# Cross-attention on one core: scores formed transposed, row maxima exchanged through DRAM

## The reference

```python
a = layer_norm(ctx, gamma, beta)                  # (32, 375, 512)
Q = heads(x @ Wq.T)                               # (32, 16, 112, 32)
K = heads(a @ Wk.T); V = heads(a @ Wv.T)          # (32, 16, 375, 32)
scores = einsum('bhtd,bhsd->bhts', Q, K) * 32 ** -0.5
attn = softmax(where(mask, scores, -inf), axis=-1)
out = merge(einsum('bhts,bhsd->bhtd', attn, V)) @ Wo.T
return x + tanh(gate) * out
```

## Time and profile before

| | us |
|---|---|
| runs (3) | 1137.56, 1139.86, 1142.44; median 1139.86 |
| span of the profiled execution, first to last instruction | 1134.9 |
| PE busy / PEld busy | 1100.3 / 921.6 |
| DVE / ACT / POOL busy | 861.4 / 679.0 / 565.0 |

### The profile page before, as it was taken

How to read it: one execution, slowest core, us unless ns; L and a number is a source line. 1 busy time by engine, 2 the same in 40 slices (tenths; PEclk the granted TensorE clock), 3 DMA queues, 4 the chain that set the end, 5 groups by cost and what they waited for, 6 DMA issues and landing times.

```text
span 1134.9 us, 28841 instructions
## 1 busy us (share of the span) xinstructions
PE 1100.3 (97%) x9614; PEld 921.6 (81%) x9614; DVE 861.4 (76%) x2438; ACT 679.0 (60%) x1811; POOL 565.0 (50%) x745
## 2 busy tenths in 40 slices
PE   9799899999999999999999999999999999999997
PEld 8798788878888888888888888888888887888885
DVE  4643888887877788888787788888787778887764
ACT  2414565656666666666666666666666666666653
POOL 1344746555555566655455566655554566655100
PEclk9899899999999999999999999999999999999997
DMA  9453223222333233323333333323333333331000
GB/s 270 168 152 70 69 73 72 55 76 74 83 85 85 72 85 73 66 64 75 77 85 85 80 77 77 70 56 75 77 85 85 82 75 76 67 67 45 10 17 17
DMA packets 53010, 89.55 MB, mean 79 GB/s; under 512 B 15184, under 2 KB 35664, under 8 KB 52976
## 3 DMA queue, kind: packets, MB, share of 16 engines
q1 hardware_dynamic: 52400, 88.19, 31.8%
q10 hardware_dynamic: 576, 0.92, 0.3%
HBM read 81.66 MB, written 7.44 MB: 79 GB/s over the span
## 4 chain that ended last, share of the span: by engine, by line
PE 72%; DVE 16%; DMA 5%; issue 4%; POOL 1%; ACT 1%; SPq 1%; DVEq 0%; POOLq 0%
PE bank L690 43%; PE bank L747 14%; PE bank L847 6%; DVE shared_f L668 6%; PE bank L770 6%; DVE stats L574 4%; DVE shared_f L649 3%; PE bank L712 2%; DMA qT<-in_wkT 2%; DMA row_stats<-row_stat 1%; DMA rows<-in_ctx 1%; DVE mv L577 1%; POOL cn L404 1%; ACT shared_f L513 1%; DMA stat_bc<-row_stats 0%
## 5 line engine op out<-in xcount | busy, mean ns | idle before, releaser
L404 POOL TENSOR_TENSOR cn<-cn,stat_bc 128x375 f32<-128x375 f32 x256 | 258.8, 1043 | 387.4 <-DMA stat_bc<-row_stats 371.1
L513 ACT ACTIVATE shared_f<-shared_f,ntop 112x375 f32<-112x375 f32 x512 | 306.3, 601 | 14.3 <-DVE ntop L649 14.1
L690 PE MATMUL bank<-shared_r,w_k 128*128 128x376 f32 x1536 | 295.9, 342 | 0.0
L690 PE MATMUL bank<-w_v,shared_r 128*125 128x512 f32 x1152 | 291.7, 402 | 0.1
L649 DVE CUSTOM_DVE_ANT_0 shared_f<-bank,mask_b 112x375 f32<-112x375 f32 x512 | 258.6, 543 | 32.1 <-PE bank L770 30.8
L690 PEld LDWEIGHTS bank<-shared_r,w_k 128*128 128x128 f32 x1536 | 260.4, 190 | 0.3
L747 PEld LDWEIGHTS bank<-ident,shared_f 112*125 112x125 f32 x1536 | 199.1, 190 | 67.9 <-issue 27.9
L690 PEld LDWEIGHTS bank<-w_v,shared_r 128*125 128x125 f32 x1152 | 206.7, 186 | 46.1 <-issue 0.5
L668 DVE TENSOR_SCALAR shared_f<-shared_f,rden 112x375 f32<-112x375 f32 x512 | 240.3, 531 | 4.5
L747 PE MATMUL bank<-ident,shared_f 112*125 112x112 f32 x1536 | 222.1, 281 | 20.2 <-DVE shared_f L668 19.6
L536 ACT ACTIVATE shared_f<-bank 125x448 f32<-125x448 f32 x256 | 139.0, 543 | 166.8 <-PE bank L747 166.8
(11 more groups left out here) (49 smaller groups left out, 816.4 us busy)
## 6 DMA issues: line engine op xcount, KB each, us to landing
rows<-in_ctx SPq DMA_DIRECT2D x32, 750.0 KB
cn<-in_ctxT SPq DMA_DIRECT2D x32, 750.0 KB, 12.2
stat_bc<-row_stats SPq DMA_DIRECT2D x32, 375.0 KB, 4.4
xy<-in_x SPq DMA_DIRECT2D x32, 224.0 KB, 2.5
out<-xy SPq DMA_DIRECT2D x32, 224.0 KB, 2.3
shared_f<-in_xT SPq DMA_DIRECT2D x7, 896.0 KB, 8.9
mask_u<-in_mask SPq DMA_DIRECT2D x32, 41.0 KB, 3.1
qT<-in_wqT SPq DMA_DIRECT2D x4, 256.0 KB, 5.5
```

Source lines behind the costliest of these rows:

```text
L404: last = pool.tensor_tensor(chunk, chunk, stat_bc[:, w, :], op)
L513: last = act.activation(prob[0:T, r % 2, h, :], prob[0:T, r % 2, h, :], ACT.Exp, bias=ntop[0:T, r % 2, h:h + 1], scale=-1.0, accum_out=den ...
L690: last = pe.matmul(dst, l, m, start=(start and k == 0), stop=(stop and k == len(pairs) - 1))
```

## The change

The scores are formed transposed: the K chunk is the stationary operand and the query the moving one, 125 context positions on the partitions by 4 x 112 query columns, for each of the three thirds j (ST = 3). They are float32 products with the operands unsplit (`kT` and `qs` lose their low parts). The exponentials are then already in the form in which the weighted sum takes them, and the weights (probabilities) are never transposed. The maximum of a query now runs over partitions and thirds. ACT copies the scores with the mask as a bias. DVE takes the maximum within each quadrant of 32 partitions (a reduction with a transposed read), SP stores these 128 x 42 numbers to DRAM and loads them back so that each partition has all twelve (four quadrants by three thirds) for its 14 queries; DVE reduces these, spreads the result over the partitions with a transposed copy, and subtracts it. ACT takes the exponentials. PE sums them over all three thirds with a matrix of ones and puts the sums beside the weighted sum; the division is made once per element, on the heads' output. The split of that output into high part and rest is also made once per element, and the output projection comes later, in a slot of the second element after. V has two banks. The mask is loaded and transposed once. Rows, context and statistics are loaded in other slots of SP than before.

The core of the diff, in the order SyncE (the exchange and its slots), ScalarE (copies and exponentials), VectorE, TensorE (scores, the sums at the end of `weighted_sum`, the slot):

```diff
+        row_max = nc.dram_tensor("row_max", (32, HC * ST * BLK), F32, kind="Internal").ap()
...
+            def exchange_maxima(i, r):
+                sync.wait_ge(quad_max, i * LOOP + r)
+                sync.dma_start(row_max.rearrange("t (q k) -> q t k", q=HC), rmax[:, :]) \
+                    .then_inc(max_stored, 16)
+                wait_apart(sync, max_stored, i * (16 * LOOP) + r * 16)
+                sync.dma_start(x4[:, :], bass.AP(
+                    tensor=row_max.tensor, offset=0,
+                    ap=[[0, HC], [HC * ST * BLK, 32], [1, HC * ST * BLK]])).then_inc(ld_max, 16)
 
             def slot(i, r):
                 c, u = divmod(r, KT)
+                if live(i, LOOP, r - 1, SLOTS):
+                    exchange_maxima(i, r)
+                if u == 0:
+                    if live(i, 2, c + 3, B) and behind(i, 2, c + 1):
+                        store_stats(i, c + 3)
+                    if live(i, 2, c - 1, B) and not first_two(i, c - 1):
+                        wait_apart(sync, stored[(c - 1) % 2], i * 16 + (c - 1) // 2 * 16)
+                        load_x(i, c - 1)
+                if u == 2:
+                    if live(i, 2, c + 3, B) and behind(i, 2, c + 1):
+                        load_stats(i, c + 3)
+                    if live(i, 2, c + 3, B) and not first_two(i, c + 3):
+                        wait_apart(sync, c_done, i * LOOP + (c + 2) * KT)
+                        load_ctx(i, c + 3)
+                if u == 3:
+                    if live(i, 2, c + 5, B) and behind(i, 2, c + 2):
+                        load_rows(i, c + 5)
+                    if live(i, 2, c - 2, B):
+                        wait_apart(sync, y_done, i * 2 + (c - 1))
+                        sync.dma_start(out[i * 2 + (c - 2), :, :], xy[0:T, c % 2, :]) \
+                            .then_inc(stored[c % 2], 16)
...
+            def scores_out(i, r):
...
+                for j in range(ST):
+                    act.activation(prob[0:SP_, (r - 1) % NB, j, :].rearrange("p (h t) -> p h t", h=HC),
+                                   sbank[0:SP_, :, T * j:T * j + T], ACT.Identity,
+                                   bias=mask_b[0:SP_, c % 2, j:j + 1]).then_inc(s_out, 1)
...
+                    for j in range(ST):
+                        act.wait_ge(sub_done, i * (LOOP * ST) + ((r - 2) * ST + j + 1))
+                        act.activation(prob[0:SP_, (r - 2) % NB, j, :], prob[0:SP_, (r - 2) % NB, j, :],
+                                       ACT.Exp, scale=SCALE).then_inc(exp_done, 1)
...
+            def row_maximum(i, r):
+                dve.wait_ge(ld_max, i * (16 * LOOP) + (r - 1) * 16)
+                dve.tensor_reduce(top[:, :], x4[:, :].rearrange("p (a k) -> p k a", k=BLK),
+                                  AX.X, ALU.max).then_inc(top_done, 1)
+                dve.wait_ge(top_done, i * LOOP + (r - 1))
+                dve.transpose(spread.rearrange("p (k a) -> p k a", a=32),
+                              top[:, :].unsqueeze(2).to_broadcast([128, BLK, 32])) \
+                    .then_inc(spread_done, 1)
+
+            def quadrant_maxima(i, r):
+                for j in range(ST):
+                    dve.wait_ge(s_out, i * (LOOP * ST) + ((r - 1) * ST + j + 1))
+                    last = dve.tensor_reduce(
+                        rmax[:, BLK * j:BLK * j + BLK],
+                        prob[:, (r - 1) % NB, j, :].rearrange("p (k a) -> p k a", a=32),
+                        AX.X, ALU.max, apply_transpose=True)
+                last.then_inc(quad_max, 1)
+
+            def subtract_maximum(i, r):
+                dve.wait_ge(spread_done, i * LOOP + (r - 1))
+                for j in range(ST):
+                    dve.tensor_tensor(prob[0:SP_, (r - 2) % NB, j, :], prob[0:SP_, (r - 2) % NB, j, :],
+                                      spread[0:SP_, :], ALU.subtract).then_inc(sub_done, 1)
...
             def slot(i, r):
+                c, u = divmod(r, KT)
                 if live(i, LOOP, r - 2, SLOTS):
+                    row_maximum(i, r)
+                if live(i, LOOP, r - 1, SLOTS):
+                    quadrant_maxima(i, r)
+                if live(i, LOOP, r - 2, SLOTS):
+                    subtract_maximum(i, r)
+                if u == 3 and live(i, 2, c - 1, B):
+                    normalise(i, c - 1)
...
+            def scores(i, r):
...
+                for j in range(ST):
+                    for h in range(HC):
+                        part = slice(HD * h, HD * h + HD)
+                        last = pe.matmul(bank[h][0:SP_, T * j:T * j + T],
+                                         kT[part, r % 2, SP_ * j:SP_ * j + SP_],
+                                         qs[part, c % 2, u, :], start=True, stop=True)
...
+                for j in range(ST):
+                    for h in range(HC):
+                        last = pe.matmul(bank[PB][HD * h:HD * h + HD, T:2 * T], ones[0:SP_, :],
+                                         prob[0:SP_, (r - 2) % NB, j, T * h:T * h + T],
+                                         start=(j == 0), stop=(j == ST - 1))
...
+            def slot(i, r):
+                if live(i, LOOP, r + 1, SLOTS):
+                    project_k(i, r)
+                vc, j = v_item(r)
+                if j is not None and live(i, 2, vc, B):
+                    project_v(i, r, vc, j)
+                if r % KT == 1 and live(i, 2, r // KT - 2, B):
+                    output(i, r)
...
+                if live(i, LOOP, r, SLOTS):
+                    scores(i, r)
+                if live(i, LOOP, r - 2, SLOTS):
...
+                    weighted_sum(i, r)
```

More of the change, by code:

```diff
@@ L137, in xattn @@
         ld_x = [sem(f"ld_x{i}") for i in range(2)]
-        ld_mask = [sem(f"ld_mask{i}") for i in range(2)]
+        ld_mask = sem("ld_mask")
         stored = [sem(f"stored{i}") for i in range(2)]
@@ L209, in slots @@
         def slots(engine, slot, first=-1, last=SLOTS // LOOP + 1):
-            for i in range(first, 1):
+            for i in range(first, 2):
                 for r in range(LOOP):
                     slot(i, r)
-            with engine.Fori(1, SLOTS // LOOP - 2) as i:
+            with engine.Fori(2, SLOTS // LOOP - 3) as i:
                 for r in range(LOOP):
                     slot(i, r)
-            for i in range(SLOTS // LOOP - 2, last):
+            for i in range(SLOTS // LOOP - 3, last):
                 for r in range(LOOP):
@@ L578, in statistics @@
                 last.then_inc(stats_done, 1)
+            def statistics(i, c):
+                bn_rows(i, c, range(ST))
+                bn_join(i, c)
             def weight_lo(n, raw, dst):
```

620 lines of the change are left out of this document (305 added, 315 removed).

## The result

The median of four runs is 1266.56 us (1263.05 to 1268.27), beside 1138.99 (1137.56 to 1142.44) for four of the kernel before: a ratio of 1.1108, with a 95% interval of 1.108 to 1.1136. The change makes the kernel 11% slower. The forecast was 1290, so 23 us too much. The profiled execution has a span of 1261.2; the median lies 5.4 above it, where 5.0 was added. Only 1.9 of the 5.4 lie around the span (that execution itself took 1263.05); the rest is that it was the fastest of the four.

What follows compares the result with a forecast made beforehand. The prediction took TensorE, 97% busy, as the present bound and a loop through the DRAM exchange as the new one: 110.1 + 127 x 9.03 + 26.2 + 5.0 = 1288, said as 1290 us, 13% slower, range 1150 to 1450.

Steps and rivals of the forecast that it cites:

- The mechanism: In every slot, one whole DRAM exchange of maxima and five VectorE instructions follow each other: 8.40 us against TensorE's 7.1.
- what was to show it: Scores about 9 us apart, TensorE about 80% busy, long wait before the small reduction, store wait 4 to 5 behind rows.
- VectorE's part: Reduction of returned maxima, spread and three quadrant reductions in each slot: 2.70 us, bounds 2.4 and 3.9.
- The rows slot: Slot 3 of an element, whose exchange follows the load of rows: the exchange loses 2.1 us.
- on SyncE's queue: A small transfer behind a large one there waits for it: 2.5 us per element, 0.63 a slot.
- The head: Time until the first scores, now behind a projection of V: 107.3 + 2.8 = 110.1 us.
- The tail: From the last scores to the end of the span, a pure chain: 26.2 us, where 20.7 was.
- (a): Exchange costs less than a slot leaves, TensorE stays the bound: 1043 us, 8% faster; faster 10%, about the same 4%.
- (b): Loop decides, large loads hardly disturb it, load back takes 2.4: step 8.2, 1183 us; 64% together with the main case.
- (c): TensorE's clock falls during its waits, 3 us per element: 96 us more, 1385; chance 12%.
- (d): Load back costs what the statistics' broadcast does, or transposed passes are half dearer: step 10.2 to 10.6, 1440 to 1490; 10%.
- an estimated 1377: Whole time if four engines moved the exchange's 84 KB load: 0.9 us of transfer instead of 0.2, 3.5 for the load.

Runs made afterwards that it cites:

- experiment 1: Kernel after without the exchange: SyncE issues neither DMA, VectorE reduces only its own quadrant's maxima; 1065.07 us, ratio 0.935 to the kernel before.
- (5): Kernel after with the store of the maxima issued twice, each waited for, before the load back; 1546.66 us in one run.
- (4): Kernel after with VectorE taking the next quadrant maxima before waiting for the previous item's exchange, two buffers; 1120.32 us, ratio 0.9839 to the kernel before.
- (11): Kernel after with the load of rows, still one DMA over 125 partitions, issued on ScalarE's queue; 1291.65 us, ratio 1.1264 to the kernel before.
- (2): Kernel after with the load of rows split over 112 and 13 partitions, to use 16 engines; 1205.69 us, ratio 1.0586 to the kernel before.
- 7: Kernel after with quadrant maxima first, two buffers, and the load of rows split over 112 and 13 partitions; 1067.43 us, ratio 0.9375 to the kernel before.
- 9: Kernel after with quadrant maxima first, double buffers, split load of rows, and two buffers for the sums of exponentials; 1055.86 us, ratio 0.9213 to the kernel before.
- 3: Kernel after with five extra identity products before each weighted sum to keep TensorE busy; 1291.51 us, ratio 1.1337 to the kernel before.
- 10: Kernel after with three extra products of 256 columns in two slots of four; 1294.18 us, ratio 1.1299 to the kernel before.
- (6): Kernel after with the load back over 128 partitions outermost, VectorE reducing only its own quadrant's maxima; 1249.05 us, ratio 1.0969 to the kernel before.

## Why the prediction was right, and where its terms were off

**The mechanism** is shown, not only argued: without the exchange the kernel takes 1065 (experiment 1), with a doubled store it pays every microsecond of it (5), and with the order of two VectorE steps turned round, 146 us go with no DMA taken away (4). It is the loop of one exchange and VectorE's steps. Of what was to show it, nearly every point came: a step of 8.8 for the 9 forecast, idle before the weighted sum behind the exponential, and a wait for the store of 2.2 in most slots and 4.2 to 4.5 behind the rows. TensorE's share was 88% for 80; at the busy time of experiment 1, nearly all at full clock, it would be 81%. The long wait before the small reduction came in three slots of four; in slot 2 the way over ScalarE is as long as the exchange, and the prediction, which laid that work beside the loop, doesn't have it.

**The sum**, cut at SyncE's first and last store: the forecast is 112.6 (110.1 and 2.45 for copies and maximum) + 127 x 9.03 + 23.8 + 5.0 = 1288. Measured: 119.1 + 127 x 8.813 + 22.9 + 5.4 = 1266.6. So the steps gave 27.6 less, the head took 6.5 more, the tail about 1 less. That the sum is within 2% is in part luck: terms with errors of either sign stand in it, below.

**The steps.** VectorE's part with SyncE's waking measured 2.74 (forecast 2.9), the store 2.24 (2.5), the load to the reduction 3.2 (3.0): together 8.2, and 8.12 in slot 0, the shortest, for 8.40. The parts of VectorE were off against each other: the reduction of 168 takes 0.447 (0.33 forecast), the transposed read 0.603 (0.62), so that bound of half dearer passes is out. Why the store of statistics, from which the 2.5 was read, took longer than this one isn't shown. The rows slot is 2.4 longer (10.50 less 8.12) for a forecast of 2.1: its store waits 1.94 more, and its load takes 3.60 to the reduction for 3.16 in slot 0. Slot 2 is 0.4 longer, the forecast's number for the context, but not by its cause: its store waits 2.27, 0.05 more than in slot 0, and the 0.36 more from load to reduction are VectorE's, held up over ScalarE. That the number fits is luck. Another 0.2 falls in slot 1, where the load takes 3.39 to the reduction with the statistics and the context issued right behind it. That is 0.74 a slot for 0.63. The step of 8.86 over an element lies a little below the middle of the 8.4 to 9.6 given for it.

**Where the delay sits** was half wrong. The prediction says that a small transfer behind a large one "on SyncE's queue" waits for it, and counts the time until the large one leaves the engines. The time was nearly right (1.94 for 2.1), the queue was not: from ScalarE's queue the rows delay the store as much (11), and over all sixteen engines from SyncE's own queue they have left before it comes (2). The Trainium skill's page "DMA: Bandwidth & Descriptors" (Issuing engines are not separate DMA queues) says that DMAs of all issuing engines run on the same 16 DMA engines and interleave; by that rule the move gains nothing, and the runs agree (4.41 for 4.38).

**The head** was 6.5 short, and this is a term that was missing. The first scores are at 110.51, as forecast (110.1). But ScalarE copies them with the mask as a bias, and that bias stood in GpSimd's order behind row statistics which waited for a load of rows. The chain of the kernel after there:

```profile
98.57 11.34 DMA rows<-in_ctx
...
109.93 1.89 DVE stats L622 x3
...
113.23 1.05 POOL rs L397
...
116.46 0.20 POOL mask_b L366
...
116.73 0.64 ACT shared_f L531
...
119.12 3.84 DMA row_max<-rmax
```

The load took 11.34 us of the chain, the copy came at 116.73 instead of 110.9, and the store at 119.12. The prediction looked at what is queued behind the exchange on SyncE, and not at what stands ahead of the new reader of the mask. Experiment 2 agrees: with the rows over sixteen engines the first store is at 105.27.

**The tail** was right in sum and not in its parts: the last scores are at 1225.69, 35.5 from the end instead of 26.2, because TensorE runs ahead of the exchange there; the last output projection took 5.46 at half clock where 4.75 was taken.

**The rivals.** (a), TensorE as the bound, is what experiments 1, 7 and 9 make: 1056 to 1067 for the 1043 worked out, mostly because TensorE's step is 7.26 (experiment 1) and not 7.1. For the kernel itself it is out: its point was a step of 7.87, and the step is 8.81. (b), a step of 8.2, would need the rows' delay gone; experiment 2 takes it away and has 8.46. (c), the clock: it fell as the rival says, once in an element behind an idle of 2.9, mean 0.935, but the time doesn't follow it: with the clock raised, the passes of experiments 3 and 10 that have no other wait take the same time within 0.3%, for the 96 us of the rival. The cause of that idle, ScalarE's wait for the one buffer of sums, was not foreseen. (d) is out, 3.2 for the load and 0.6 for the passes. The Trainium skill's rule on the leading dimension ("DMA: Bandwidth & Descriptors", Rules for kernel authors) says how many engines a DMA gets and not what that costs; the 0.7 us a load by which the prediction had an estimated 1377 didn't come true for the exchange, where another leading dimension gave 0.35 with the shorter issue (6). For the rows, with five engines, it was worth 61 us (2).

## What to carry to other kernels

A round trip that one engine both feeds and waits for is a loop: its length is the round trip plus all that stands between the wait and the next feed, and it must be held against the step of the busiest engine. Before shortening the trip, look whether the feed can be moved ahead of the wait; here that and a second buffer were worth 146 us, and half a microsecond off the load and its reduction 17. A large DMA over few of the engines delayed small ones from either of the two queues tried, so split it to use all engines before moving it. A step that only fills idle time also lengthens a program: look at the page's instruction packets when waits without a releaser come up. And when an operand gets a new first reader, follow what stands ahead of its producer in the prologue too.

## What the runs showed of the hardware that was not expected

- A store of 21 KB in tiny pieces and the load back of 84 KB take 2.2 and 3.2 us here from issue to the waiting instruction. For the load, the number of engines hardly matters (3.2 with a leading dimension of 4, 2.9 with 128, of which 0.18 is the issue); for the store it wasn't tried.
- In two kernels whose program for TensorE was longer within the loop (13,969 and 13,073 instructions in all instead of 12,689), TensorE stood 4 to 5 us without a releaser, once per pass of the loop and ten times in the whole execution. The kernel after has none. They had 132 and 129 packets on the instruction queue instead of 38, nearly all of the surplus in the passes with these waits.
- In the kernel after, the granted clock was at half for 6.8 us around and behind an idle of 2.9 us in one element, and for 3.4 in three beside it, while TensorE was busy again, and then went back to full.
